# Layer 1's x lays: one 512 KB transfer each instead of four (or two)

## The chip, the core and the metric

The kernel runs on one core of one Trainium2 chip. The metric is device time in microseconds, as the median of a few runs. A profiled execution has a time of its own, and inside it a span, from its first to its last instruction. The names of the engines are those of the profile: PE (TensorE, matmuls), PEld (its weight loads), DVE (VectorE), ACT (ScalarE), POOL (GpSimd) and SP (SyncE, which here only issues transfers). Transfers are carried out by the core's 16 DMA engines. KB in this text is 1024 bytes, MB a million bytes, GB/s a thousand MB per second.

## What is computed

For a batch of 2048, 39 embedding rows of 16 numbers are gathered from tables (x0). Two layers of pairwise products follow, and a small tower on top:

```
z0 = einsum('bid,bjd->bdij', x0, x0).reshape(B, D, 39 * 39)
cur0 = relu(einsum('bdk,kl->bld', z0, W0))            # 128 outputs
next_h, direct0 = split(cur0, 2, axis=1)              # 64 + 64
z1 = einsum('bid,bjd->bdij', x0, next_h).reshape(B, D, 39 * 64)
cur1 = relu(einsum('bdk,kl->bld', z1, W1))
z = sum(concatenate([direct0, cur1], axis=1), axis=-1)
h = concatenate([z, dense_ctx], axis=1)
y = relu(relu(h @ W_top1 + b_top1) @ W_top2 + b_top2) @ W_top3
```

The output needs every product of a row of x0 with a row of next_h (z1), summed over W1; that is where the lays come in.

## The kernel before

The work is cut into 32 units (`UNITS`): 16 tiles of 128 batch rows, each in two halves of 8 of the 16 dimensions. One unit has C = 1024 columns (8 dimensions by 128 batch rows), so a row of x of one unit is 4 KB.

POOL gathers a tile's embeddings, ACT spreads them, PE transposes them, and the 60 rows of x (39, some of them again) of a unit are stored to `x_rows` in device memory. SP stores the first three units' (`store_x`), ACT the other 29 (`keep_x`). Each store goes as two transfers of 120 KB: 60 rows, each in four pieces of 128 numbers, so the source in SBUF is 60x4x128 and the destination 240 runs of 128.

From `x_rows` SP loads all operands, with rows repeated as the products want them:

- Layer 0 (7 steps a unit): `load_base` fills `bases` (117 rows from a source of 39 rows by 3 copies, and 9 rows more from a source of 3x3), `load_more` fills `x_ring` and `x_more` (126 rows from a source of 42x3), `load_halves` fills `half_a` and `half_b` in runs of 49, 15, 10, 39 and 15 rows of half a width.
- Layer 1 (20 steps a unit): ten **lays** a unit, `lay(u, m)`, m = 0 to 9. A lay is 128 rows by 1024 columns, 512 KB. Lay 0 holds two rows of x, 64 copies of each; lays 1 to 9 hold four rows of x, 32 copies each. DVE multiplies each lay of 1 to 9 twice, once with each of two tiles `h_quad` (L902, steps k = 0 and 1), and lay 0 once with `h_pair`. The step between them (HALF1) uses `x_last` instead, which SP loads in two transfers of 64 rows.

Before the change, a lay is loaded by one transfer for each of its rows of x: four of 32x1024 (128 KB), or for lay 0 two of 64x1024 (256 KB). The source of each is one row repeated, 32x1024 or 64x1024, with the same shape as its destination.

There are six slots for lays (`NX` = 6). SP may issue lay n only when DVE has made the last product of lay n - 6 (`sp.wait_ge(z_made, ...)`), and DVE waits for the slot's semaphore to reach 16 for every transfer into it so far (`lay_parts`). The order of SP's queue is written out by hand in its `body(u)`: lays 6 to 9 of unit u, lay 0 of u + 1, base and more loads of u + 2 with lay 1 of u + 1 in between, `x_last` and lay 2 of u + 1, the halves of u + 2, and lays 3 to 5 of u + 1. A wait on SP holds up everything behind it.

PE takes DVE's products in order (L493 plain; L511, L514 and L518 for steps whose product ACT and DVE split in two; L501 for the halves). DVE waits for PE only when its four buffers of plain products are full.

Of the kernel before, what the change touches and what calls it, by code (L numbers as in the profile page):

```python
# [5 lines left out]
P = 128  # L6
# [4 lines left out]
H = L // 2  # L11
# [4 lines left out]
C = DH * P  # L16
# [15 lines left out]
FQ = 9  # L32
STEPS1 = 2 + 2 * FQ
LAYS = 1 + FQ
# [12 lines left out]
NX = 6  # L47
# [5 lines left out]
QUAD = P // 4  # L53
# [25 lines left out]

def lay_parts(n):  # L80

    return sum(2 if k % LAYS == 0 else 4 for k in range(n % NX, n + 1, NX))


def gathers(t):
# [4 lines left out]
def quad_step(m, k):  # L90

    q = 2 * (m - 1) + k
    return 1 + q + (1 + q >= HALF1)
# [17 lines left out]
def at1(u, s):  # L111

    return STEPS0 + STEPS * u + s + sum(a < s for a in after(u))
# [22 lines left out]
def tower(nc, ids, tables, hot_ids, hot_tables, hot_consts, ident_in, dense_t, w0_a, w0_b, w1_whole, w1_split, top, top_small, y):  # L136
    ctx = ExitStack()
    with ctx:
# [8 lines left out]
        def sem(name):  # L147
            return ctx.enter_context(nc.semaphore(name))


        x_rows = nc.dram_tensor("x_rows", [UNITS, RING, C], FP, kind="Internal").ap()
# [70 lines left out]
        def lay(u, m):  # L222
            n = (LAYS * u + m) % NX
            return x_lay[:, n * C:(n + 1) * C]
# [62 lines left out]
        lay_loaded = [sem(f"lay_loaded{n}") for n in range(NX)]  # L287
# [44 lines left out]
        def _(sp):  # L332
# [28 lines left out]
            def load_lay(u, m):  # L361
                n = LAYS * u + m
                if n >= NX:
                    pu, pm = divmod(n - NX, LAYS)
                    sp.wait_ge(z_made, at1(pu, quad_step(pm, 1) if pm else 0) + 1)
                reps = H if m == 0 else QUAD
                for a in range(P // reps):
                    row = 4 * FQ + a if m == 0 else 4 * (m - 1) + a
                    src = x_rows[u, row:row + 1, :].to_broadcast([reps, C])
                    sp.dma_start(lay(u, m)[a * reps:(a + 1) * reps, :], src).then_inc(lay_loaded[n % NX], 16)  # L370

            def load_last(u):
                if u >= 1:
# [5 lines left out]
            def body(u):  # L379
                more_follow = u < UNITS - 2  # L380
                load_lay(u, 6)
                load_lay(u, 7)
                load_lay(u, 8)
                load_lay(u, 9)
                if u + 1 < UNITS:
                    load_lay(u + 1, 0)
                if u == 0:
                    store_x(2)
                    load_lay(1, 1)
                if more_follow:  # L390
                    sp.wait_ge(x_stored, 32 * (u + 2) + 32)
                    load_base(u + 2, 0)
                    load_more(u + 2, 0)
                    load_more(u + 2, 1)
                if 0 < u < UNITS - 1:
                    load_lay(u + 1, 1)
                if more_follow:
                    load_base(u + 2, 1)
                    load_more(u + 2, 2)
                if u + 1 < UNITS:  # L400
                    load_last(u + 1)
                    load_lay(u + 1, 2)
                if more_follow:
                    load_halves(u + 2)
                if u + 1 < UNITS:
                    for m in range(3, 6):
                        load_lay(u + 1, m)
# [481 lines left out]
        def _(dve):  # L889
# [44 lines left out]
            def step1(u, s):  # L934
                if s == HALF1:
                    dve.wait_ge(last_loaded, 32 * u + 32)
                    dve.wait_ge(h_half_made, u + 1)
                    make(at1(u, s), h_half, x_last)
                    return
                m, k = lay_part(s)  # L940
                n = LAYS * u + m
                if k == 0:
                    dve.wait_ge(lay_loaded[n % NX], 16 * lay_parts(n))
                if s == 0:
                    dve.wait_ge(h_pair_made, u + 1)
                    if u == 0:
                        dve.wait_ge(pair_copied, 2)
                elif m == 1:
                    if u == 0 and k == 0:
                        for j in range(4):  # L950
                            relu_copy(h_quad[0][0][j * QUAD:(j + 1) * QUAD, BANK:C], slice(0, QUAD), quad_copied)
                        dve.wait_ge(quad_copied, 4)
                    dve.wait_ge(h_quad_made[k], u + 1)
                make(at1(u, s), h_quad[u % 2][k] if s else h_pair, lay(u, m))
# [311 lines left out]
```

## Time and profile before

| | us |
|---|---|
| median of 3 runs | 1515.13 (1511.45 to 1517.09) |
| profiled execution | 1511.94 |
| its span | 1510.1 |
| PE busy | 1434.6 (95%) |
| DVE busy | 1393.3 (92%) |
| ACT busy | 825.2 (55%) |
| POOL busy | 939.0 (62%) |
| queue of SP's transfers (q1): share of the 16 DMA engines' span | 77.2%, 278.48 MB |

A time in this table says how long an engine had work, not that it set the end. The profile also has a chain of waits (the work that ended last, followed back), the waits of each engine with what released it, the busy share of every engine in any stretch, and the transfers: how many packets and bytes each queue moved, and how many packets were small.

### The profile page before, as it was taken

How to read it: one execution, taken by the hardware profiler on the slowest of the kernel's cores; microseconds unless marked ns; L12 is line 12 of the kernel's file. 1: busy time of each engine (PE TensorE's matmuls, PEld its weight loads, DVE VectorE, ACT ScalarE, POOL GpSimd, SP SyncE). 2: the span in 40 equal slices, each digit the busy share in tenths (PEclk: the TensorE clock that was granted, in tenths of full speed). 3: DMA queues.
4: the chain of work that ended last, by engine and by line, in shares of the span. 5: the costliest groups of instructions: out<-in, count | busy, mean ns of one | idle time of the engine just before them, and what ended most of it. 6: DMA issues, size and time to landing. Idle time of an engine off the chain costs nothing.

```text
span 1510.1 us, 15015 instructions
## 1 busy us (share of the span) xinstructions
PE 1434.6 (95%) x4458; PEld 794.5 (53%) x4458; DVE 1393.3 (92%) x1253; ACT 825.2 (55%) x897; POOL 939.0 (62%) x604
## 2 busy tenths in 40 slices
PE   3179999999999999999999999999999999999999
PEld 2145555555555555555555555555555555555556
DVE  2179999999999999999999999999999999999993
ACT  0155555655655555655655555655655555655555
POOL 7638888868687786868687786868687780000000
PEclk7589999999999999999999999999999999999999
DMA  5069989999989899999989999899998998898510
GB/s 150 6 160 203 227 216 218 206 220 212 221 198 222 206 217 214 208 223 201 220 203 216 214 212 220 208 213 203 212 216 223 212 210 216 204 222 207 170 35 1
DMA packets 137289, 293.08 MB, mean 194 GB/s; under 512 B 37646, under 2 KB 62878, under 8 KB 137080
## 3 DMA queue, kind: packets, MB, share of 16 engines
q1 hardware_dynamic: 102642, 278.48, 77.2%
q0 software_dynamic: 19200, 4.95, 2.9%
q10 hardware_dynamic: 15366, 8.70, 2.1%
q8 instruction: 35, 0.57, 0.2%
q14 instruction: 46, 0.38, 0.1%
HBM read 284.08 MB, written 7.87 MB: 193 GB/s over the span
## 4 chain that ended last, share of the span: by engine, by line
PE 90%; DVE 4%; issue 2%; another core or an unknown queue 2%; ACT 0%; DMA 0%; DVEq 0%; SPq 0%
PE psB L493 42%; PE psA L493 14%; PE psB L511 7%; PE psB L514 6%; PE psB L518 6%; PE psA L501 2%; PE psA L511 2%; PE psA L514 2%; PE psA L518 2%; PE psB L501 2%; DVE z L902 1%; PE psA L485 1%; DVE z_lo L911 1%; DVE z_split L902 1%
## 5 line engine op out<-in xcount | busy, mean ns | idle before, releaser
L472 POOL DMA_INDIRECT emb<-in_tbl,ids_all x600 | 938.8, 1565 | 309.7 <-issue 178.9
L493 PE MATMUL psB<-z,w 128*128 128x512 f32 x1544 | 690.1, 593 | 5.3 <-DVE z L902 5.3
L767 ACT ACTIVATE z_hi<-z_split 128x1024 fp32r<-128x1024 f32 (+1 forms) x286 | 301.4, 1057 | 464.9 <-DVE z_split L902 372.4
L493 PEld LDWEIGHTS psB<-z,w 128*128 128x128 f32 x1544 | 292.4, 190 | 362.7 <-issue 346.0
L902 DVE TENSOR_TENSOR z<-h_quad,x_lay 128x1024 f32<-128x1024 f32 x354 | 420.5, 1218 | 7.4 <-PE psB L493 5.4
L911 DVE TENSOR_TENSOR z_lo<-z_split,z_hi 128x1024 fp32r<-128x1024 f32 (+1 forms) x286 | 349.3, 1221 | 6.3 <-ACT z_hi L767 3.2
L902 DVE TENSOR_TENSOR z_split<-h_quad,x_lay 128x1024 f32<-128x1024 f32 x222 | 268.4, 1221 | 0.0
L720 ACT ACTIVATE h_quad<-psA 32x1024 f32<-32x1024 f32 x248 | 251.7, 1015 | 6.1 <-DVE feat_side L987 2.4
L493 PE MATMUL psA<-z,w 126*128 126x512 f32 x512 | 241.9, 594 | 0.0
L511 PE MATMUL psB<-z_hi,w_hi 128*128 128x512 f32 x444 | 157.7, 436 | 0.0
L493 PEld LDWEIGHTS psA<-z,w 126*128 126x128 f32 x512 | 97.3, 190 | 98.4 <-issue 92.7
L518 PE MATMUL psB<-z_lo,w_hi 128*128 128x512 f32 x444 | 138.2, 392 | 1.8 <-DVE z_lo L911 1.7
L514 PE MATMUL psB<-z_hi,w_lo 128*128 128x512 f32 x444 | 138.8, 394 | 0.0
L902 DVE TENSOR_TENSOR z<-bases,x_more 126x1024 f32<-126x1024 f32 x96 | 116.7, 1216 | 0.0
L511 PEld LDWEIGHTS psB<-z_hi,w_hi 128*128 128x128 f32 x444 | 78.7, 188 | 50.4 <-issue 39.3
L518 PEld LDWEIGHTS psB<-z_lo,w_hi 128*128 128x128 f32 x444 | 81.0, 188 | 25.2 <-DVE z_lo L911 6.2
L514 PEld LDWEIGHTS psB<-z_hi,w_lo 128*128 128x128 f32 x444 | 83.3, 188 | 19.1
L758 ACT ACTIVATE r<-psB 128x1024 f32<-128x1024 f32 x32 | 32.8, 1025 | 66.1 <-issue 53.5
L712 ACT ACTIVATE h_pair<-psA 64x1024 f32<-64x1024 f32 x62 | 63.2, 1020 | 6.8 <-PE psA L501 4.3
L511 PE MATMUL psA<-z_hi,w_hi 126*128 126x512 f32 x128 | 53.1, 496 | 0.0
L698 ACT ACTIVATE x_side<-psA 120x512 f32<-120x512 f32 x32 | 19.2, 600 | 60.8 <-PE psA L485 29.3
L902 DVE TENSOR_TENSOR z<-h_pair,x_lay 128x1024 f32<-128x1024 f32 x32 | 38.9, 1216 | 4.8 <-PE psB L493 3.5
(113 smaller groups left out, 862.5 us busy)
## 6 DMA issues: line engine op xcount, KB each, us to landing
x_lay<-x_rows SPq DMA_DIRECT2D x1152, 128.0 KB
x_more<-x_rows SPq DMA_DIRECT2D x62, 504.0 KB
bases<-x_rows SPq DMA_DIRECT2D x62, 468.0 KB
x_lay<-x_rows SPq DMA_DIRECT2D x64, 256.0 KB
x_ring<-x_rows SPq DMA_DIRECT2D x31, 504.0 KB
emb<-in_tbl,ids_all POOLq DMA_INDIRECT x600
x_last<-x_rows SPq DMA_DIRECT2D x64, 128.0 KB
x_rows<-x_side ACTq DMA_DIRECT2D x58, 120.0 KB
```

What stands on the lines that cost most here:

```text
L472: nc.gpsimd.indirect_dma_start(emb[t % 2][:, f * D:(f + 1) * D], None, tables[f], bass.IndirectOffsetOnAxis(ids_all[:, t, f:f + 1], 0)).th ...
L493: mm = nc.tensor.matmul(ps[:, cs], w[0:k, :], z[WHOLE_NO[place] % NZ][0:k, cs], start=first, stop=last)
L501: mm = nc.tensor.matmul(ps[:, n * BANK:(n + 1) * BANK], w[rows, :], z[WHOLE_NO[place] % NZ][rows, 0:BANK], start=False, stop=last)
L511: nc.tensor.matmul(ps[:, cs], w_hi[0:k, :], z_hi[n % NS][0:k, cs], start=first, stop=False)
L514: nc.tensor.matmul(ps[:, cs], w_lo[0:k, :], z_hi[n % NS][0:k, cs], start=False, stop=False)
L518: mm = nc.tensor.matmul(ps[:, cs], w_hi[0:k, :], z_lo[n % NS][0:k, cs], start=False, stop=last)
L712: op = nc.scalar.activation(h_pair[n * H:(n + 1) * H, :], h[0:H, :], ACT.Relu)
L720: op = nc.scalar.activation(h_quad[u % 2][k][n * QUAD:(n + 1) * QUAD, :], h[k * QUAD:(k + 1) * QUAD, :], ACT.Relu)
L758: nc.scalar.activation(r1_by_b[:, :, u % 2 * DH:(u % 2 + 1) * DH], by_d, ACT.Relu).then_inc(relu1_done, 1)
L767: nc.scalar.activation(z_hi[n % NS][0:k, 0:cols], z_split[n % NS][0:k, 0:cols], ACT.Copy).then_inc(z_hi_made, 1)
L902: nc.vector.tensor_tensor(out[0:k, 0:cols], a[0:k, 0:cols], b[0:k, 0:cols], ALU.mult).then_inc(z_made, 1)
L911: nc.vector.tensor_tensor(z_lo[n % NS][0:k, 0:cols], z_split[n % NS][0:k, 0:cols], z_hi[n % NS][0:k, 0:cols].bitcast(FP), ALU.subtract).th ...
```

## The change

Each lay is loaded by one transfer. Its source is written as a pattern of three dimensions, rows by copies by columns: 4x32x1024 for lays 1 to 9 and 2x64x1024 for lay 0; the destination is the slot's 128 partitions by 1024. The same bytes are read and written. `lay_parts` now counts one transfer for each use of a slot.

```diff
 def lay_parts(n):
 
-    return sum(2 if k % LAYS == 0 else 4 for k in range(n % NX, n + 1, NX))
+    return n // NX + 1
...
-                reps = H if m == 0 else QUAD
-                for a in range(P // reps):
-                    row = 4 * FQ + a if m == 0 else 4 * (m - 1) + a
-                    src = x_rows[u, row:row + 1, :].to_broadcast([reps, C])
-                    sp.dma_start(lay(u, m)[a * reps:(a + 1) * reps, :], src).then_inc(lay_loaded[n % NX], 16)
+                reps, row = (H, 4 * FQ) if m == 0 else (QUAD, 4 * (m - 1))
+                src = x_rows[u, row:row + P // reps, :].unsqueeze(1).to_broadcast([P // reps, reps, C])
+                sp.dma_start(lay(u, m), src).then_inc(lay_loaded[n % NX], 16)
```

No other engine's instructions move. On SP's queue, one unit's worth in the middle of the program before the change, from the load of `x_last` to lay 1 of the next unit but one (sizes are the destination's):

```order
L377 DMA x_last<-x_rows 64x512 x2
L370 DMA x_lay<-x_rows 32x1024 x4
L357 DMA half_a<-x_rows 49x512 x2
L357 DMA half_a<-x_rows 15x512 x2
L357 DMA half_b<-x_rows 10x512 x2
L357 DMA half_b<-x_rows 39x512 x2
L357 DMA half_b<-x_rows 15x512 x2
L370 DMA x_lay<-x_rows 32x1024 x28
L370 DMA x_lay<-x_rows 64x1024 x2
L341 DMA bases<-x_rows 117x1x1024
L342 DMA bases<-x_rows 9x1x1024
L347 DMA x_ring<-x_rows 126x1x1024
```

And the same place on SP's queue after the change:

```order
L375 DMA x_last<-x_rows 64x512 x2
L368 DMA x_lay<-x_rows 128x1x1024
L357 DMA half_a<-x_rows 49x512 x2
L357 DMA half_a<-x_rows 15x512 x2
L357 DMA half_b<-x_rows 10x512 x2
L357 DMA half_b<-x_rows 39x512 x2
L357 DMA half_b<-x_rows 15x512 x2
L368 DMA x_lay<-x_rows 128x1x1024 x8
L341 DMA bases<-x_rows 117x1x1024
L342 DMA bases<-x_rows 9x1x1024
L347 DMA x_ring<-x_rows 126x1x1024
```

The order is the same; 28 + 2 transfers became 8 (lays 3 to 5, then 6 to 9, and lay 0), and 4 became 1 (lay 2).

## Rows read from the trace of the kernel before

**Rows 1.** The page: PE's busy time; DMA busy share in 40 slices.

```profile
PE 1434.6 (95%) x4458; PEld 794.5 (53%) x4458; DVE 1393.3 (92%) x1253; ACT 825.2 (55%) x897; POOL 939.0 (62%) x604
...
DMA  5069989999989899999989999899998998898510
```

**Rows 2.** Stretches: busy time of each engine, granted clock, DMA share, GB/s.

```profile
core 0: us, PE busy (x) PEld busy (x) DVE busy (x) ACT busy (x) POOL busy (x), PEclk, DMA share, GB/s
40.00:60.00 20.00, 2.08 (x8) 1.78 (x8) 6.74 (x7) 4.36 (x6) 15.12 (x17) 0.50 0.07 7
...
83.30:1439.70 1356.40, 1350.04 (x4144) 737.35 (x4143) 1328.89 (x1171) 781.26 (x837) 886.93 (x546) 1.00 0.90 211
```

**Rows 3.** Waits: SP (whole span), then DVE and PE (100 to 1410 us).

```profile
engine line waited for: us in total, times, longest us
SPq L370 <- DVE z L902: 269.4, 117, 5.7
...
DVE z L902 <- DMA x_lay<-x_rows: 0.2, 1, 0.2
...
PE psB L493 <- DVE z L902: 5.3, 3, 3.0
```

**Rows 4.** The page, DMA issues: tile, queue, count, KB each.

```profile
x_lay<-x_rows SPq DMA_DIRECT2D x1152, 128.0 KB
x_more<-x_rows SPq DMA_DIRECT2D x62, 504.0 KB
bases<-x_rows SPq DMA_DIRECT2D x62, 468.0 KB
x_lay<-x_rows SPq DMA_DIRECT2D x64, 256.0 KB
x_ring<-x_rows SPq DMA_DIRECT2D x31, 504.0 KB
...
x_last<-x_rows SPq DMA_DIRECT2D x64, 128.0 KB
x_rows<-x_side ACTq DMA_DIRECT2D x58, 120.0 KB
half_a<-x_rows SPq DMA_DIRECT2D x62, 98.0 KB
...
bases<-x_rows SPq DMA_DIRECT2D x62, 36.0 KB
```

**Rows 5.** DMA from 78.0 to 83.2 us: packets, and what was issued.

```profile
DMA packets 510, 0.25 MB, mean 47 GB/s; under 512 B 30, under 2 KB 510, under 8 KB 510
...
x_rows<-x_side SPq DMA_DIRECT2D x2, 120.0 KB
```

**Rows 6.** The page, DMA totals, and queues: packets, MB, share of 16 engines.

```profile
DMA packets 137289, 293.08 MB, mean 194 GB/s; under 512 B 37646, under 2 KB 62878, under 8 KB 137080
...
q1 hardware_dynamic: 102642, 278.48, 77.2%
q0 software_dynamic: 19200, 4.95, 2.9%
q10 hardware_dynamic: 15366, 8.70, 2.1%
```

**Rows 7.** Stretches, columns as in rows 2: last two DMA share, GB/s.

```profile
88.00:96.00 8.00, 8.00 (x35) 4.76 (x33) 7.31 (x7) 6.43 (x10) 1.03 (x2) 1.00 1.04 234
1432.00:1439.00 7.00, 7.00 (x22) 3.79 (x21) 7.00 (x7) 3.15 (x3) 0.00 (x0) 1.00 1.05 243
103.00:106.00 3.00, 1.95 (x4) 0.68 (x4) 2.91 (x5) 2.93 (x6) 2.41 (x2) 1.00 0.85 287
...
1429.00:1431.00 2.00, 2.00 (x7) 0.82 (x5) 2.00 (x2) 1.93 (x2) 0.00 (x0) 1.00 0.97 396
```

**Rows 8.** Timeline: start, us, work. SP's first lay load; DVE's last lay products.

```profile
83.30 1.14 SPq L370 DMA_DIRECT2D x_lay<-x_rows  x2
...
1455.67 2.36 DVE L902 TENSOR_TENSOR z<-h_quad,x_lay 128x1024 f32<-128x1024 f32 x2
```

## The prediction

> **What bounds the kernel now.** I read the page's busy times first, then the stretches, then the waits. PE is busy 95% of the span, and DMA stands near 9 tenths in nearly every slice [rows 1]. The stretch from the first lay load to the end of the last one says it better: of 1356.4 us PE is busy 1350.0, at a granted clock of 1.00 (the higher of its two levels, 2.4 GHz), with the DMA engines at 0.90 and 211 GB/s [rows 2]. So PE sets the time, and the DMA engines are close behind it: there is little room in them. The waits confirm it. Between 100 and 1410 us DVE waited 0.2 us for a lay, and PE's longest group of waits for DVE is 5.3 us; it is SP that waits, 269.4 us, for slots to come free, since lays are there ahead of their use [rows 3].
>
> From this the change can hardly bring anything. What it could save is issue time on SP, an engine that waits for slots anyway, and DMA time, for which nobody waits. All that PE could get back in the stretch is 1356.4 - 1350.0 = 6.4 us. So the question is what one transfer of this shape does to the DMA engines.
>
> **How many DMA engines carry a transfer.** From 78.0 to 83.2 us the only transfers issued are two stores of x, each from a source of 60x4x128 to 240 runs of 128 numbers. The trace has 510 packets, 30 of them under 512 B [rows 5]. The data are 2 x 240 = 480 packets; the 30 small ones are 15 for each store. I read a small packet as one DMA engine's report that its part is done: 15 engines, not 16, though the destination's 240 would divide by 16. 60, the outer size of the source, does not divide by 16 but by 15. ACT's queue holds 58 such stores and four table loads of 128 rows, which I count with 16 engines each: 58 x (240 + 15) + 4 x (128 + 16) = 15366, the row's number exactly [rows 6]; with 16 for a store it would be 15424.
>
> The same count over all of SP's transfers, each with one packet for every destination row and one report for each of the largest number of engines up to 16 that divides both outer sizes, gives 75786 + 26856 = 102642, again the row's number exactly [rows 6]. In it the 62 loads of 9 rows from a source of 3x3 (36 KB, [rows 4]) count 3 engines; with 9, as the destination alone would allow, the sum would be 372 too high. So the outer size of the source decides here, although 3x3 rows lie behind it.
>
> The Trainium skill says the same: "DMA: Bandwidth & Descriptors", section "Why a DMA increments its semaphore by 16 and not by 1", takes the largest k up to 16 that divides the slowest dimension of both patterns, and its section "Rules for kernel authors" warns of an outermost dimension below 16; the trace agrees, with its 15 and its 3. The rule in the same section to coalesce small transfers into large ones speaks for the change and would give no loss, about 1512 us; nothing waits for the lays [rows 3], so no gain either.
>
> Are the engines of a narrow transfer always the same ones? From 103 to 106 us the queue is filled with base, ring and more loads alone, of 13 and 14 engines by this count. The DMA share there is 0.85, against 1.04 and 1.05 where it is full of 16-engine lay loads [rows 7]. 13/16 and 14/16 are 0.81 and 0.875. If successive transfers started on other engines the idle ones would fill; they do not. So a fixed set.
>
> **The change, part by part.**
>
> - Removed: 1152 transfers of 128 KB and 64 of 256 KB [rows 4], 16 engines each. Added: 288 transfers of 512 KB with a source of 4x32x1024, and 32 with 2x64x1024. By the count above the first run on 4 engines and the second on 2.
> - Bytes on the busiest two engines. Lays 1 to 9: 288 x 512/4 = 36864 KB. Lay 0: 32 x 512/2 = 8192 KB. Unchanged ones [rows 4]: bases 62 x 468/13 = 2232 and 62 x 36/3 = 744; x_more and x_ring 93 x 504/14 = 3348; the halves 62 x (14 + 2 + 2 + 6 + 2) = 1612 (49 rows of 2 KB over 7 engines make 14 KB, the other four runs likewise); x_last 64 x 8 = 512; stores 64 x 8 = 512; the top weights 80; gathers 4.95 MB / 16, about 300 [rows 6]. Together 54,400 KB, 55.7 MB. Before, an engine carried 293.08 / 16 = 18.3 MB on average [rows 6]; this is three times as much on two engines, while twelve have a quarter of their work left.
> - Rate of one engine. No stretch of before shows four engines alone. The nearest rows are: lays alone, 234 and 243 GB/s over 16 engines, 14.6 and 15.2 each; base, ring and more loads, 287 / (16 x 0.85) = 21.1 each; the load of the top weights, with every partition another row, 396 / (16 x 0.97) = 25.5 each [rows 7]. I take 21.1. These loads are the nearest in form: a three-dimensional source in which each engine reads rows of its own, as the four engines of a new lay would, while in the old lay loads sixteen read the same 4 KB. The ends of the range are 14.6 and 25.5.
> - Time for them: 55.7 MB / 21.1 GB/s = 2640 us.
> - Is that queue always full? SP asks for lay n + 6 when lay n has been used, so five lays lie in the queue, 5 x 0.131 MB / 21.1 = 31 us of work, more than any step of SP's hand-written order takes. SP's wait for slots stays and grows; behind it on its queue stand base, more and halves of a unit whose turn comes a unit later. So nothing empties the two engines until the last lay.
> - Who waits: DVE for lays, and PE for DVE. PE's 1350 us of work lie beside the 2640. Where PE is mostly idle its granted clock is 0.50 (40 to 60 us, 2.08 of 20 us busy, [rows 2]), its 1.2 GHz level. If it stayed there throughout, its work would be 2 x 1350 = 2700 us, about the same as the transfers', so I add nothing. It does put a brake on a result far below 2640.
> - Ends: 83.3 us before the first lay load, and from DVE's last products of a lay (1455.7) to the end of the span, 1510.1 - 1455.7 = 54.4 us [rows 8]. They are unchanged, if the clock is high at the end.
> - Removed issue: 1216 - 320 = 896 instructions on SP, at nothing, as its waits cover them.
>
> Sum: 83.3 + 2640 + 54.4 = 2778 us of span, and 1.8 us around it (1511.94 against 1510.1): **2780 us**. The profiled execution is 3 us below the median of the runs, which is nothing beside this.
>
> **Rivals.**
>
> 1. Two engines in each other's way: 3500 us. The four engines of a lay advance side by side, with the 32 rows of each quarter, and share something where they write. Then the rate of lays 1 to 9 is that of the old lay loads, 14.6 to 15.2 each [rows 7]: 37.75 MB / 15.2 = 2483 or, at 14.6, 2586 us; the other 17.95 MB at 21.1 take 851; with the ends 3475 to 3575. For it: lays are the slowest loads in the trace per engine. Against it: sixteen engines loaded them, and two of a pair may drift apart. The Trainium skill, "SBUF — State Buffer", section "Door 1: The DMA port swizzle", says that partitions 0 to 31 and 32 to 63 lie behind the same eight of 16 ports; quarters 1 and 2 would be such a pair, and its 27.2 GB/s for a port would give 13.6 for an engine. By that figure, an estimate, the sum would be some 3770.
> 2. Four engines with the memory to themselves: 25.5 GB/s as for the top weights [rows 7]. 55.7 / 25.5 = 2184, with the ends 2324 us. Against it: PE's clock, above.
> 3. The transfers are not narrowed, or over nine engines or more carry them: about 1510 us, no change. The point where it decides: PE needs 1356 / 32 = 42.4 us for a unit, in which an engine at 21.1 moves 0.895 MB; 0.30 MB of it go to other loads, so the lays' 5.24 MB a unit need 5.24 / 0.595 = 8.8 engines. This would be so if the repeated dimension (step 0) were merged with the 128 partitions. Against it: the bases' 39 rows by 3 copies are such a source, and the count holds with 13 for them.
> 4. Rival 3 with all of the 6.4 us that PE idles in the stretch won back [rows 2]: 1505 us, faster by about 0.5%. Against it: DVE's wait for lays is 0.2 us in all [rows 3].
>
> **Chances.** The forecast (rates around 21) has 0.45, rival 1 0.28, rival 2 0.18, rival 3 0.07, rival 4 0.02. The range takes the forecast and rivals 1 and 2 whole: 2320 to 3700; left out are rivals 3 and 4 and something like 0.05 above. A measurement of this kernel can tell about 0.5% from no change; slower by more than that 0.91, within it 0.07, faster 0.02.
>
> **What would show it.** In the profile after: SP's queue with 288 x (128 + 4) + 32 x (128 + 2) packets for lays where 1152 x 48 + 64 x 80 were, so 102642 - 18240 = 84402 in all; a DMA share of about a quarter to a third with 100 to 110 GB/s; DVE waiting for x_lay over 1000 us; PE's share near a half, and its clock below 1.00 in many slices; lay loads that take some 6 us each at the head of the queue. Wrong would be the count, if the packets are 288 x 144 + 32 x 144; then rival 3 holds. If the count holds and the time does not, the rate of one engine is the term that was mis-sized.

## The result

The changed kernel takes 2438.52 us (median of 4 runs, 2432.7 to 2445.29) against 1516.11 us (median of 4 runs): a ratio of 1.607, with a 95% interval of 1.598 to 1.616. It is slower by 61%. The forecast was 2780 us with a range of 2320 to 3700; the side, the mechanism and the range held, the time was forecast 14% too high (a loss of 1265 us against the measured 922).

The page of the changed kernel, first its busy times, slices and packets, then its queues (packets, MB, share of the 16 engines' span):

```profile
span 2438.3 us, 14119 instructions
...
PE 1717.2 (70%) x4458; PEld 850.3 (35%) x4458; DVE 1411.4 (58%) x1253; ACT 825.8 (34%) x897; POOL 728.4 (30%) x604
...
PEclk6798888889988888988888998889888888889879
DMA  3244343433334343333433333343333333333330
...
DMA packets 119042, 292.95 MB, mean 120 GB/s; under 512 B 19406, under 2 KB 44638, under 8 KB 118840
...
q1 hardware_dynamic: 84402, 278.40, 32.9%
q0 software_dynamic: 19200, 4.95, 2.0%
q10 hardware_dynamic: 15366, 8.70, 1.2%
```

These answer to [rows 1] and [rows 6]. SP's queue moved the same bytes (278.40 MB against 278.48) with 84402 packets, which is the number that follows from 4 engines for a lay and 2 for lay 0. The DMA share fell from 9 tenths to 3 or 4, and yet the transfers are now what everything waits for: that is what a few busy engines among many idle ones look like in a share over 16. PE is busy 283 us longer than before for the same 4458 matmuls, as its granted clock stands below 1.00 (0.866 in the mean).

The chain that ended last has changed hands from PE to DMA. By engine before, then by engine and by line after:

```profile
PE 90%; DVE 4%; issue 2%; another core or an unknown queue 2%; ACT 0%; DMA 0%; DVEq 0%; SPq 0%
...
DMA 68%; issue 10%; SPq 7%; PE 6%; DVE 6%; another core or an unknown queue 2%; ACT 1%; DVEq 0%; ACTq 0%
DMA x_lay<-x_rows 53%; DMA bases<-x_rows 12%; SPq L357 3%; DMA x_ring<-x_rows 3%; SPq L341 3%; DVE z L900 2%; PE psB L491 2%; DVE z_split L900 2%; SPq L368 1%; PE psA L491 1%; DVE z_lo L909 1%; DMA x_rows<-x_side 1%; PE psB L516 1%; DVE feat_d L960 1%
```

And the waits over the whole span, which answer to [rows 3] (who waited <- for what: us in total, times, longest):

```profile
DVE z L900 <- DMA x_lay<-x_rows: 461.2, 131, 9.9
...
PE psB L491 <- DVE z L900: 328.7, 97, 14.8
...
DVE z_split L900 <- DMA x_lay<-x_rows: 151.9, 67, 4.3
```

DVE waited 461.2 + 151.9 = 613 us for lays where it had waited 0.2, and PE waited for DVE. The last link is what one engine moves. Three stretches of the changed kernel (columns as in [rows 2]): lays 1 to 9 alone, a lay 0 alone, and base and other wide loads.

```profile
642.00:650.00 8.00, 6.07 (x23) 3.82 (x22) 8.00 (x8) 2.29 (x3) 6.78 (x5) 1.00 0.29 108
657.50:660.50 3.00, 3.00 (x13) 2.24 (x12) 2.57 (x4) 2.95 (x4) 0.92 (x1) 1.00 0.16 55
604.00:606.00 2.00, 0.03 (x1) 0.06 (x1) 1.23 (x1) 0.00 (x0) 1.70 (x2) 0.59 0.89 288
```

108 GB/s over four engines and 55 over two are 27 GB/s for each, at shares of 0.29 and 0.16, near 4/16 and 2/16. The gathers, which use all 16 engines, are in these figures. SP's queue alone moved 0.83 MB in the first stretch and took 25.2% of the 16 engines' time, which is four engines at 26 GB/s. I go on with 27; it is some 4% high. The wide loads still go at 288 GB/s, as in [rows 7].

### The profile page after: what moved, and what is told of

Its sections match the earlier page's. It is cut to its first block, busy times and chain, and to the rows that moved or that the text cites. A ratio compares the mean times of both kernels' runs of the same rounds, so it can differ in the third digit from the quotient of the medians.

```text
span 2438.3 us, 14119 instructions
## 1 busy us (share of the span) xinstructions
PE 1717.2 (70%) x4458; PEld 850.3 (35%) x4458; DVE 1411.4 (58%) x1253; ACT 825.8 (34%) x897; POOL 728.4 (30%) x604
## 3 DMA queue, kind: packets, MB, share of 16 engines
q1 hardware_dynamic: 84402, 278.40, 32.9%
## 4 chain that ended last, share of the span: by engine, by line
DMA 68%; issue 10%; SPq 7%; PE 6%; DVE 6%; another core or an unknown queue 2%; ACT 1%; DVEq 0%; ACTq 0%
DMA x_lay<-x_rows 53%; DMA bases<-x_rows 12%; SPq L357 3%; DMA x_ring<-x_rows 3%; SPq L341 3%; DVE z L900 2%; PE psB L491 2%; DVE z_split L900 2%; SPq L368 1%; PE psA L491 1%; DVE z_lo L909 1%; DMA x_rows<-x_side 1%; PE psB L516 1%; DVE feat_d L960 1%
## 5 line engine op out<-in xcount | busy, mean ns | idle before, releaser
L491 PE MATMUL psB<-z,w 128*128 128x512 f32 x1544 | 818.8, 673 | 397.6 <-DVE z L900 328.7
L470 POOL DMA_INDIRECT emb<-in_tbl,ids_all x600 | 728.2, 1214 | 1228.9 <-ACT emb_spread L688 1048.3
L491 PEld LDWEIGHTS psB<-z,w 128*128 128x128 f32 x1544 | 312.6, 210 | 841.4 <-issue 606.3
L900 DVE TENSOR_TENSOR z_split<-h_quad,x_lay 128x1024 f32<-128x1024 f32 x222 | 270.5, 1220 | 187.8 <-DMA x_lay<-x_rows 151.9
L491 PE MATMUL psA<-z,w 126*128 126x512 f32 x512 | 282.9, 681 | 53.2 <-DVE z L900 38.0
L516 PE MATMUL psB<-z_lo,w_hi 128*128 128x512 f32 x444 | 172.8, 475 | 157.9 <-DVE z_lo L909 107.8
L491 PEld LDWEIGHTS psA<-z,w 126*128 126x128 f32 x512 | 110.5, 222 | 196.6 <-issue 187.1
L512 PE MATMUL psB<-z_hi,w_lo 128*128 128x512 f32 x444 | 150.5, 423 | 0.0
L900 DVE TENSOR_TENSOR z<-bases,x_ring 126x1024 f32<-126x1024 f32 x32 | 39.3, 1229 | 124.3 <-DMA x_ring<-x_rows 77.5
L512 PEld LDWEIGHTS psB<-z_hi,w_lo 128*128 128x128 f32 x444 | 90.8, 204 | 22.1
L516 PE MATMUL psA<-z_lo,w_hi 126*128 126x512 f32 x128 | 45.6, 439 | 15.8 <-DVE z_lo L909 15.0
```

Source lines behind the costliest of these rows:

```text
L470: nc.gpsimd.indirect_dma_start(emb[t % 2][:, f * D:(f + 1) * D], None, tables[f], bass.IndirectOffsetOnAxis(ids_all[:, t, f:f + 1], 0)).th ...
L491: mm = nc.tensor.matmul(ps[:, cs], w[0:k, :], z[WHOLE_NO[place] % NZ][0:k, cs], start=first, stop=last)
L512: nc.tensor.matmul(ps[:, cs], w_lo[0:k, :], z_hi[n % NS][0:k, cs], start=False, stop=False)
L516: mm = nc.tensor.matmul(ps[:, cs], w_hi[0:k, :], z_lo[n % NS][0:k, cs], start=False, stop=last)
L900: nc.vector.tensor_tensor(out[0:k, 0:cols], a[0:k, 0:cols], b[0:k, 0:cols], ALU.mult).then_inc(z_made, 1)
```

## The experiments

They ran on three chips on which the kernel before takes 1476 or 1477 us instead of 1516, and the first lay of these runs is loaded at some 40 us instead of 83.3; the ends (before the first lay load, after the last lay, around the span) are therefore 96 us instead of 139.5. The first experiment gives the changed kernel on one of them, and everything below is compared with that. Each time is the median of four runs, but six experiments are single runs and say so. Where an edit changes the number of transfers for a lay, the counts in `lay_parts` change with it, which the cuts of code do not show.

**The changed kernel again.** No edit.

> The changed kernel once more, beside the kernel before on the chip of these experiments, where the kernel before takes 1476 us, its first 80 us being some 40 shorter. If that opening is all that differs, 2400 us; with it the runs that left out work are compared.

Measured: 2402.79 us, ratio 1.628 (1.625 to 1.631). With 46.1 MB of lays at 27 GB/s, 1709 us, and 96 for the ends, 598 us are left for the other 9.6 MB of a busiest engine. This is the split with which the next runs are read: ends 96, lays by their rate, rest 598.

**The same transfer with its copies outermost.**

```diff
-                src = x_rows[u, row:row + P // reps, :].unsqueeze(1).to_broadcast([P // reps, reps, C])
+                src = x_rows[u, row:row + P // reps, :].unsqueeze(0).to_broadcast([reps, P // reps, C])
```

> Changed kernel, but the source of each lay is written with its copies outermost: 32 copies x 4 rows x 1024 (lay 0: 64 x 2 x 1024) instead of 4 x 32 and 2 x 64. Still one transfer of 512 KB for each lay, the same rows of x and the same bytes; the rows land interleaved in the slot, so the products are of other pairs than the reference's. Theory N (a transfer runs on the largest number of engines up to 16 that divides the outer sizes, so 4 or 2 in the changed kernel, and 16 here): 288 x 144 + 32 x 144 packets for the lays, 88308 on SP's queue; DMA no longer the bound, 1505 to 1520 us. Rival L (one large transfer with a repeated dimension inside is slow or lands too late, whatever its outer size): stays near 2438 us.

Measured: 1475.05 us, ratio to the kernel before 0.9995 (0.9981 to 1.0009). SP's queue and a long stretch of it:

```profile
q1 hardware_dynamic: 88306, 278.42, 67.3%
...
100.00:1370.00 1270.00, 1267.11 (x3871) 690.80 (x3868) 1249.11 (x1095) 730.37 (x775) 873.71 (x535) 1.00 0.78 212
```

One transfer of 512 KB, the same three-dimensional pattern, the same bytes, two sizes exchanged: the whole loss is gone, and the packets are the count for 16 engines (320 x 144 for the lays; 88308 in the expectation was a slip of addition). So the cause is the outer size, and not the size of the transfer or its repeated dimension. (The rows of x land interleaved in the slot there, so this kernel leaves out the right pairing; the bytes and the work of the computing engines are the same.) It also settles that nothing is to be had here: the DMA share falls from 0.90 to 0.78, and the time stays, as PE is busy for 1267 of 1270 us.

**Eight rows outermost.**

```diff
-                reps, row = (H, 4 * FQ) if m == 0 else (QUAD, 4 * (m - 1))
+                reps, row = (16, 4 * FQ) if m == 0 else (16, 4 * (m - 1))
```

> Changed kernel, but each lay, lay 0 too, is read as 8 rows x 16 copies x 1024 (other rows than the reference's, the same 512 KB). N: 8 engines; the busiest carry 320 x 64 KB = 21.0 MB of lays and 9.6 MB of the rest, 30.5 MB; at the 24.2 GB/s that the changed kernel's span gives for an engine (55.7 MB in 2301 us) that is 1261 us, under PE's 1350, so 1510 to 1570 us, at the edge. L: near 2438 us.

Measured: 1628.28 us, ratio 1.102 (1.097 to 1.107), above both figures of N, and far from L. SP's queue has 85746 packets, the count for 8 engines. The direction with the number of engines is right, the rate was not. A stretch of lay loads:

```profile
624.00:636.00 12.00, 9.66 (x32) 5.08 (x31) 8.43 (x8) 5.11 (x7) 9.53 (x9) 1.00 0.59 184
```

184 GB/s at a share of 0.59, near 8/16: 23 GB/s for each of eight engines, not 27. 21.0 MB / 23 = 913, and 913 + 598 + 96 = 1607 us, 1.3% under the measurement. (SP's queue alone moved 2.12 MB there, 22 GB/s for each; with it the sum is 1643 us, 0.9% over.) My turning point of 8.8 engines was computed with 0.30 MB a unit for the rest at 21.1; the rest costs 598 us, not 453, which moves it up, to nine or ten engines.

**Two rows outermost, two transfers for a lay.**

```diff
-                src = x_rows[u, row:row + P // reps, :].unsqueeze(1).to_broadcast([P // reps, reps, C])
-                sp.dma_start(lay(u, m), src).then_inc(lay_loaded[n % NX], 16)
+                for a in range(1 if m == 0 else 2):
+                    src = x_rows[u, row + 2 * a:row + 2 * a + 2, :].unsqueeze(1).to_broadcast([2, reps, C])
+                    sp.dma_start(lay(u, m)[2 * a * reps:2 * (a + 1) * reps, :], src).then_inc(lay_loaded[n % NX], 16)
```

> Lays 1 to 9 by two transfers of 256 KB, each with a source of 2 rows x 32 copies (correct data); lay 0 as in the changed kernel. N: everything on two engines, 75.5 + 8.4 MB of lays and 9.6 of the rest; at 27 GB/s for the lays (107 to 113 GB/s over four engines in the changed kernel) 3107 us, with the 590 that the rest then left and 140 for the ends 3840 us; at 24.2 for everything 4000. L: smaller transfers, nearer to before: between 1512 and 2438 us.

Measured: 3821.63 us (a single run). It loads the same rows as the changed kernel in transfers half as large, and it is 59% slower than that. Read with the split above: 83.9 MB / 27 = 3107, + 598 + 96 = 3801 us. This also shows that all narrow transfers use the same engines: had the two transfers of a lay gone to different pairs, the time would have been that of the changed kernel. The two busiest engines carry 37.75 MB more than in the changed kernel, and the time is 1419 us longer: 26.6 GB/s for one engine, without any stretch having been chosen.

**Lay 0 alone merged, and lays 1 to 9 alone merged.**

```diff
+                if m == 0:
+                    src = x_rows[u, 4 * FQ:4 * FQ + 2, :].unsqueeze(1).to_broadcast([2, H, C])
+                    sp.dma_start(lay(u, m), src).then_inc(lay_loaded[n % NX], 16)
+                    return
                 for a in range(P // QUAD):
                     src = x_rows[u, 4 * (m - 1) + a:4 * (m - 1) + a + 1, :].to_broadcast([QUAD, C])
```

> Lay 0 alone by one transfer (2 x 64 x 1024), lays 1 to 9 in four parts as before. N: the two busiest engines carry 8.4 MB for lay 0, 9.4 for lays 1 to 9 and 9.6 of the rest, 27.4 MB; at 21 GB/s 1300 us, under PE's 1350, but each lay 0 holds two engines for 256 KB / 27 = 9.7 us while the queue behind it waits: 1515 to 1600 us. At the slowest rates of each kind (15 for parts) up to 1670. L: a tenth of the loss, 1512 + 92 = 1600 us.

Measured: 1757.19 us, ratio 1.191 (1.189 to 1.192). A single narrow transfer a unit costs 281 us, nearly 9 for each, more than either figure. The other one, the reverse edit:

```diff
+                if m:
+                    src = x_rows[u, 4 * (m - 1):4 * m, :].unsqueeze(1).to_broadcast([4, QUAD, C])
+                    sp.dma_start(lay(u, m), src).then_inc(lay_loaded[n % NX], 16)
+                    return
                 for a in range(2):
                     src = x_rows[u, 4 * FQ + a:4 * FQ + a + 1, :].to_broadcast([H, C])
```

> Lays 1 to 9 by one transfer each (4 x 32 x 1024), lay 0 in two parts of 64 rows as before. N: four engines carry 37.7 MB of lays 1 to 9 and lay 0's 1.05, where two had 8.4 MB of lay 0: 7.3 MB less on the busiest, at 27 GB/s 272 us less than the changed kernel, 2165 us (with 24.2 GB/s 303 less, 2135). L (loss by number of merged lays, nine tenths of it): 2345 us.

Measured: 2184.17 us (a single run), 219 less than the changed kernel (272 were expected by N, 93 by L, a tenth of the loss): lay 0, a tenth of the bytes, has nearly a quarter of the 927 us of loss, as two engines and not four carry it. By the split: 37.7 / 27 = 1398, lay 0's 1.05 MB at 15 another 70, + 598 + 96 = 2162.

For lay 0 alone the split gives 8.4 / 27 = 311 for it, and for the old lay parts 9.4 MB at the rate of this run's own stretch of them,

```profile
648.00:658.00 10.00, 5.50 (x19) 2.79 (x18) 4.91 (x5) 2.12 (x2) 8.16 (x7) 1.00 1.05 216
```

216 / 16 = 13.5 GB/s, 699 us: 311 + 699 + 598 + 96 = 1704 us, 3% short. Two theories for what is missing were tried.

**Lay 0 issued on ACT's queue.** If the narrow transfer at the head of SP's queue keeps the wide ones behind it from the other 14 engines, another queue should help.

```diff
+                    if s == 9 and u + 1 < UNITS:
+                        act.wait_ge(x_stored, 32 * (u + 2))
+                        act.wait_ge(z_made, at1(u, quad_step(4, 1)) + 1)
+                        src = x_rows[u + 1, 4 * FQ:4 * FQ + 2, :].unsqueeze(1).to_broadcast([2, H, C])
+                        act.dma_start(lay(u + 1, 0), src).then_inc(lay_loaded[LAYS * (u + 1) % NX], 16)
```

> As the run with lay 0 alone merged (1757 us), but lay 0 of each unit after the first is issued by ACT on its own queue. The bytes on the two busiest engines stay 27.4 MB. If the narrow transfer cost so much because it holds up SP's queue, whose transfers for all 16 engines stand behind it and cannot overtake (so the other 14 engines run dry), the time falls to 1500 to 1620 us. If two engines with 27.4 MB are the limit wherever it is issued, it stays within 2% of 1757 us.

Measured: 1765.78 us, ratio 1.198 (1.195 to 1.201): no help. The transfer did move (ACT's queue has 24.96 MB instead of 8.70), and DVE now waits for it once a unit:

```profile
DVE z L907 <- DMA x_lay<-x_rows: 280.3, 33, 13.5
...
q10 hardware_dynamic: 19396, 24.96, 5.3%
```

With lay 0 on SP's queue DVE did not wait for lay 0 between 590 and 660 us, but 2 to 3 us at a time for other lays, `bases` and `x_ring`. Here these waits are nearly gone, and all of the wait is for lay 0: it is issued at 615.3 us and used at 645.6, though its rows need 10 us on two engines. So freeing the queue gives nothing back, as the time is lost at lay 0 instead. That speaks for the bytes on the two engines, which both queues use, as the limit. It does not exclude the held-up queue as part of the time of the run before, since the wait for lay 0 is new in this one.

**Lay 0 merged, with less work for PE.**

```diff
                 for c in range(C // BANK):
                     cs = slice(c * BANK, (c + 1) * BANK)
-                    nc.tensor.matmul(ps[:, cs], w_hi[0:k, :], z_hi[n % NS][0:k, cs], start=first, stop=False)
-                for c in range(C // BANK):
-                    cs = slice(c * BANK, (c + 1) * BANK)
-                    nc.tensor.matmul(ps[:, cs], w_lo[0:k, :], z_hi[n % NS][0:k, cs], start=False, stop=False)
-                pe.wait_ge(z_lo_made, n + 1)
-                for c in range(C // BANK):
-                    cs = slice(c * BANK, (c + 1) * BANK)
-                    mm = nc.tensor.matmul(ps[:, cs], w_hi[0:k, :], z_lo[n % NS][0:k, cs], start=False, stop=last)
+                    mm = nc.tensor.matmul(ps[:, cs], w_hi[0:k, :], z_hi[n % NS][0:k, cs], start=first, stop=last)
+                pe.wait_ge(z_lo_made, n + 1)
                 mm.then_inc(z_used, 1)
```

> As the run with lay 0 alone merged (1757 us), with the second and third pair of matmuls of each split step left out (PE's work falls by some 480 us, from about 1435 to about 1000). If the two busiest engines alone set the 1757 us, it stays within 1%. If the time above their bytes (27.4 MB: 9.4 and 8.4 of lays at 15 and 27 GB/s, and 600 us for the rest, 1540 us and 96 for the ends, 1636) comes from stretches in which PE is the late one and the engines find no free slot, it falls to 1640 to 1700 us.

Measured: 1767.02 us, ratio 1.197 (1.194 to 1.200): PE has no part in it. The remaining 3% stay open; DVE's wait for a slot's data and SP's wait for a slot alternate in this run, but no run isolates that.

**The changed kernel with less work for PE.** The same edit as above in the changed kernel.

> Changed kernel; of the three pairs of matmuls of each split step PE does only the first, high times high (the two with a low part are left out; DVE and ACT still make the low parts). PE's work falls by 284 x 4 matmuls of some 0.43 us, about 480 us. If the transfers alone set the time (N), it stays at 2438 us within 1%. If PE's low clock and the chain from DVE to PE have a part in the 250 us by which the time is over 55.7 MB at 27.2 GB/s, it falls by up to that, to 2190 us or more.

Measured: 2405.69 us (a single run), where the changed kernel takes 2402.79. With 1144 matmuls fewer the time is the same, so PE and its clock set nothing that can be measured in the changed kernel. Its page shows why PE is still busy for so long:

```profile
PE 1588.8 (66%) x3314; PEld 664.9 (28%) x3314; DVE 1412.3 (59%) x1253; ACT 826.9 (34%) x897; POOL 750.7 (31%) x604
```

A quarter of the matmuls are gone, and PE's busy time is 129 us less (1717.5 on this chip), as the mean granted clock went from 0.874 to 0.777. The expectation had taken some 480 us of work away at one clock.

**The other loads made tiny.**

```diff
-                sp.dma_start(more[t][0:ROWS, :], ring(u, SH * t, ROWS)).then_inc(more_loaded[t], 16)
+                sp.dma_start(more[t][0:16, 0:16], x_rows[u, 0:16, 0:16]).then_inc(more_loaded[t], 16)
```

and likewise in `load_base` and `load_halves`.

> Changed kernel; base, ring, more and half loads bring only 16 columns (bases, ring and more only 16 rows too), so that layer 0's operands are stale after unit 0; lays, x_last, stores and gathers are whole. This prices the other loads on the busiest engines, 7.9 MB of 55.7. If an engine always moves 27 GB/s they are worth 295 us: 2145 us. If it is the others that were slow (the 590 us left when the lays go at 27), and the gathers and stores keep some 80 of it: 1930 us. If the rate of 21.1 of the prediction holds for them: 375 us, 2065 us.

Measured: 2034.96 us (a single run), 368 less. The loads taken away are 7936 KB or 8.13 MB on a busiest engine (the sum of their terms in the prediction; 7.9 in the expectation was KB read as MB): 22.1 GB/s, close to the 21.1 that I had read from [rows 7]. So of the 598 us of the rest, 368 belong to 8.1 MB and 230 to the last 1.4 MB: gathers, stores, `x_last`, and whatever gaps there are. In the changed kernel on this chip the gathers' queue takes 2.9% of the span of 2403 us, 70 us for 0.3 MB of each engine, and the queue of ACT's stores 1.2%, 29 us. The others, some 130 us, are not told apart; some 65 of them are the lays' own if one engine moves 26 GB/s and not 27.

**What slowed the old lay loads.** Two kernels, to find why one engine moved 15 GB/s there and 27 in the changed kernel. The kernel before with 32 different rows as the source of each part of lays 1 to 9,

```diff
-                    src = x_rows[u, row:row + 1, :].to_broadcast([reps, C])
+                    src = x_rows[u, 0:reps, :] if m else x_rows[u, row:row + 1, :].to_broadcast([reps, C])
```

> The kernel before, but each 32x1024 part of lays 1 to 9 reads 32 different rows of x instead of one row 32 times (other data, same bytes, same 16 engines, same 32 partitions). To be read in the stretch at the opening where lays 1 to 4 are loaded alone, 230 to 240 GB/s in the kernel before. If sixteen engines reading one 4 KB row slowed them, 300 GB/s and more; if it is that the 16 engines write into 32 partitions, still 240. Time 1476 us either way, as PE sets it.

and the changed kernel with one row as the source of all 128 partitions:

```diff
-                src = x_rows[u, row:row + P // reps, :].unsqueeze(1).to_broadcast([P // reps, reps, C])
+                src = x_rows[u, row:row + 1, :].to_broadcast([P, C])
```

> The changed kernel, but each lay is one row of x for all 128 partitions (128 x 1024 from one row repeated; other data, same bytes, 16 engines). In the stretch where lays are loaded alone: if one row as the source is the limit, 240 GB/s as in the kernel before; if the 32 partitions were, 320 GB/s or more, as with the copies outermost. Time 1476 us.

Measured: 1476.7 and 1474.95 us (single runs). The stretches in which the opening's lays are loaded, of these two and of the run with the copies outermost, in this order:

```profile
46.00:53.00 7.00, 7.00 (x28) 4.41 (x26) 4.94 (x5) 4.27 (x7) 6.09 (x4) 1.00 1.05 231
...
43.00:47.00 4.00, 4.00 (x19) 2.68 (x18) 4.00 (x5) 3.93 (x7) 3.39 (x3) 1.00 0.96 320
...
43.00:50.00 7.00, 7.00 (x30) 4.21 (x29) 6.36 (x6) 5.78 (x9) 5.78 (x5) 1.00 1.01 350
```

Thirty-two different rows into 32 partitions: 231 GB/s, as with one row [rows 7]. One row into 128 partitions: 320; four rows into 128: 350, or 338 in the same four microseconds (43 to 47 us). So the shared row was not what slowed the old loads, and the reason that I gave for setting their rate aside was wrong. What is left is the transfer into 32 partitions. It was also four times smaller (128 KB against 512), and no run separates the two; but the share stands at 1.05 in the first stretch, so the engines did not wait for the next transfer. The Trainium skill, "SBUF — State Buffer", section "Door 1: The DMA port swizzle", says that 32 partitions reach half the ports. The traces agree in direction; its asymptote of 218 GB/s for them is below the 231 measured here and the 243 of [rows 7], in stretches in which transfers into all four quarters of a slot follow each other.

## Why the prediction was right, and where it was off

- **The bound before.** Right. With 16 engines kept, the one-transfer form gives a ratio of 0.9995: SP's issue time and DMA time were worth nothing.
- **The count of engines.** Right, to the packet: 84402 on SP's queue, as forecast, and by experiment 1475, 1628, 2403 and 3822 us for outer sizes of 32, 8, 4 and 2 (lay 0's is 64, 8, 2 and 2). Rival 3 (no narrowing) falls.
- **The same engines every time.** Read from shares of 0.85; right by the run with two transfers of outer size 2, which is slower than one of outer size 4.
- **The bytes on the busiest two.** 55.7 MB, right as far as the packets tell; lays 1 to 9 alone gave 2184 where the bytes ask for 2162. One remark beside the sum was wrong: the twelve other engines keep not a quarter but some two fifths of their work, since the lays were 10.5 of the 18.3 MB of an engine. Nothing in the forecast hung on it.
- **The rate of one engine, 21.1 GB/s for everything.** This is the term that was mis-sized. Lays went at 27, so their 46.1 MB cost 1709 us and not 2187: 478 us too much. The other 9.6 MB cost 592 us (2301 - 1709) and not 453: 139 too little. 2640 - 478 + 139 gives the 2301 us measured between the ends; that the second error took back part of the first was luck. (At 26 for the lays the two are 412 and 73.) The choice of row was the mistake, for the lays: I took the row nearest in the form of its source, but it had 13 or 14 engines at work at once. Lay loads went at 26 to 27 for one engine with two or four at work, at 22 to 23 with eight, and at 22 with sixteen over 128 partitions (350 / 16). The number of engines at work is not the whole reason, since the load of the top weights had 25.5 with sixteen [rows 7], and no run says what made it faster.
- **The queue always full.** Right in effect, wrong in its picture. I had five lays lying in the queue and SP free. In fact SP is held in the issue instruction itself (below); its waits for slots grew as forecast, from 390 to 692 us. Of the 900 stretches of 1 us between 300 and 1200 us one alone moved less than 40 GB/s, so the two engines hardly ever ran dry.
- **PE's clock.** It fell, to 0.866 in the mean, and cost nothing, as the run with less PE work shows. It was no brake at 2438 either, though I had argued one against rival 2: PE's clock stood at 1.00 where it was busy for 6.07 of 8 us (642 to 650 us above), and PE was busy for 1648 of the 2301 us, not 2700.
- **The ends.** Right: DVE's last lay product at 2385.0 us, the end at 2438.3, 53 us against 54.4.
- **Rival 1, engines in each other's way** (0.28, some 3500 us), falls: four engines at 26 to 27 each leave no room for it. The 13.6 GB/s, my estimate from the Trainium skill's "SBUF — State Buffer", section "Door 1: The DMA port swizzle", for engines that share a port, is not seen. **Rival 2** (25.5 GB/s, 2324 us) was nearer to the measured time than my forecast was; it had the lays nearly right (25.5 against 26 to 27) and the rest too fast, at 375 us where it cost 592.
- **What I said the profile would show.** DVE waiting for x_lay over 1000 us: it was 613, and 774 in the run again; another 96 us went to x_ring and bases, which stand behind lays in the queue, and 172 before products have no releaser in the profile. PE's share near a half: 70%, because of its clock. 100 to 110 GB/s in the mean: 120. A lay in 6 us: 4.9 by the rate (131 KB at 27).

## What to carry to other kernels

Before merging transfers, look at the outer size of both patterns as they are written, the source's above all: it decides how many of the 16 DMA engines work, and an outer size of 2 or 4 made this kernel 61% slower with the same bytes in a quarter of the instructions. The packet counts of a profile tell it, since each transfer leaves one small packet for every engine that it uses. Copies outermost, 32 or 64 of them, kept all 16 engines, but the rows then land interleaved, so the other operand must be laid out the same way; here it would have gained nothing over the four small transfers (1475 us against 1476). A low DMA share is no sign of room: four engines of sixteen that never rest read as 0.3.

## What the runs showed of the hardware that I had not expected

An instruction that issues a transfer is held on SP while narrow transfers are queued. Lay loads of the changed kernel, and of the run with copies outermost (duration in ns: least, median, most):

```profile
L368 SPq DMA_DIRECT2D x_lay<-x_rows x320: 3/3332/10058, 83.3 to 2360.1; - x160
...
L368 SPq DMA_DIRECT2D x_lay<-x_rows x320: 512/513/622, 40.5 to 1397.8; - x160
```

Both issue 320 transfers of 512 KB; with 16 engines the instruction takes 0.51 us, with 4 or 2 it takes 3.3 in the median and up to 10, as long as a lay 0 needs (262 KB at 27 GB/s are 9.7 us). With 8 engines it takes 0.63 in the median and up to 4.1; where nearly all lay transfers use two engines, 4.8 and up to 14.9. It is not the narrow instruction itself that is slow: where lay 0 alone was merged, its issue took 0.56 to 0.60 us. A lay puts 32 or 64 rows on an engine in the changed kernel, and 8 with sixteen engines, so I read it as an engine's queue that has no room, but no run varied that alone.

Second, the engines did not slow each other when few worked: 26 to 27 GB/s each with two and with four. Which rows of a slot each of the four fills, the traces do not show.
